# The second and third bf16 parts of layer 0's Q and K: VectorE instead of GpSimd, in a two-layer transformer kernel

## What is computed

```python
# layer 0, for x (8, 512, 256) and condition (8, 256)
mod = silu(condition) @ Wada + bada
sh_a, sc_a, gt_a, sh_m, sc_m, gt_m = split(mod, 6)
xm = layernorm(x, g1, be1) * (1 + sc_a) + sh_a
x  = x + gt_a * (causal_attention(xm @ Wqkv, 16 heads) @ Wproj + bproj)
xm = layernorm(x, g2, be2) * (1 + sc_m) + sh_m
x  = x + gt_m * (gelu(xm @ W1 + b1) @ W2 + b2)
# layer 1, for hidden = x and w = condition
h  = sln(hidden, w)                      # gamma(w) * layernorm(hidden) + beta(w)
q, k, v = h @ Wqkv.T + bqkv              # 16 heads, no mask
out = (softmax(q @ k.T) / 16) @ v @ Wp.T + bp
h1 = out + hidden
result = sln(h1, w) + h1
```

## Time and profile before

| what | value |
|---|---|
| median of three runs | 1229.31 us |
| lowest, highest | 1226.33, 1229.5 us |
| the profiled execution's own time | 1228.83 us |
| its span, first to last instruction | 1227.1 us |
| PE busy | 1167.0 us (95%) |
| DVE busy | 849.4 us (69%) |
| ACT busy | 656.0 us (53%) |
| POOL busy | 280.1 us (23%) |

### The profile page before, as it was taken

How to read it: one execution, slowest core, us unless ns; L and a number is a source line. 1 busy time by engine, 2 the same in 40 slices (tenths; PEclk the granted TensorE clock), 3 DMA queues, 4 the chain that set the end, 5 groups by cost and what they waited for, 6 DMA issues and landing times.

```text
span 1227.1 us, 17995 instructions
## 1 busy us (share of the span) xinstructions
PE 1167.0 (95%) x6462; PEld 587.2 (48%) x6462; DVE 849.4 (69%) x1620; ACT 656.0 (53%) x1184; POOL 280.1 (23%) x379
## 2 busy tenths in 40 slices
PE   9888999999999999999999999999999999999996
PEld 6444644454444634455445643446445463445333
DVE  4835689448984688826987388855798468764784
ACT  1262355746456555556565465565645655653664
POOL 1232221302331113301242013320232101310012
PEclk8899999999899999999999998999989999999998
DMA  5503032304232052300523023320323204300401
GB/s 201 175 9 96 21 119 39 104 18 117 56 90 66 18 137 62 102 26 30 156 56 103 19 76 93 81 78 19 110 59 87 72 1 126 80 18 16 116 20 43
DMA packets 59186, 89.31 MB, mean 73 GB/s; under 512 B 12914, under 2 KB 23762, under 8 KB 59098
## 3 DMA queue, kind: packets, MB, share of 16 engines
q1 hardware_dynamic: 57550, 86.83, 25.3%
q10 hardware_dynamic: 1548, 1.33, 0.4%
HBM read 24.41 MB, written 4.70 MB: 24 GB/s over the span
## 4 chain that ended last, share of the span: by engine, by line
PE 71%; DVE 15%; SPq 5%; ACT 4%; DMA 3%; issue 2%; POOL 1%; ACTq 0%; DVEq 0%; POOLq 0%
PE X L1097 16%; PE OP L993 12%; PE X L1028 10%; PE SC L1005 10%; PE X L1154 9%; PE X L1128 8%; DVE MX L797 6%; SPq L440 4%; ACT E L656 2%; DVE XN L847 2%; PE X L1031 2%; PE X L1112 1%; DVE PART L883 1%; DMA RS<-OE 1%; DVE STAT L804 1%
## 5 line engine op out<-in xcount | busy, mean ns | idle before, releaser
L797 DVE TENSOR_REDUCE MX<-X 128x1 f32<-128x512 f32 (+3 forms) x864 | 516.4, 660 | 170.3 <-PE X L1031 100.8
L656 ACT ACTIVATE E<-SC 128x512 f32<-128x512 f32 (+1 forms) x864 | 438.6, 592 | 278.0 <-PE SC L1005 238.0
L1028 PE MATMUL X<-KS,QS 96*128 96x512 bf16 (+3 forms) x1024 | 278.5, 349 | 16.6 <-DVE MX L797 11.6
L1005 PE MATMUL SC<-QS,KS 99*128 99x512 bf16 (+3 forms) x1024 | 261.3, 343 | 15.8 <-ACT E L656 11.1
L993 PE MATMUL OP<-E,V 128*32 128x512 f32 (+3 forms) x2048 | 212.3, 531 | 0.7 <-POOL E L565 0.4
L1005 PEld LDWEIGHTS SC<-QS,KS 99*128 99x128 bf16 x1024 | 89.7, 98 | 170.4 <-ACT E L656 89.1
L1028 PEld LDWEIGHTS X<-KS,QS 96*128 96x128 bf16 x1024 | 93.0, 98 | 147.5 <-DVE MX L797 67.4
L565 POOL TENSOR_SCALAR_AFFINE_SELECT E<-E 128x512 f32<-128x512 f32 x128 | 90.8, 717 | 223.9 <-ACT E L656 223.9
L1154 PE MATMUL X<-XT,W 128*128 128x512 f32 x256 | 117.0, 602 | 1.2 <-ACT XT L687 1.2
L1128 PE MATMUL X<-XT,WQKV 128*128 128x512 f32 x256 | 115.8, 596 | 1.3 <-ACT XT L687 1.2
L1097 PE MATMUL X<-W,HID 128*128 128x256 f32 x512 | 114.0, 380 | 0.1
(11 more groups left out here) (96 smaller groups left out, 936.7 us busy)
## 6 DMA issues: line engine op xcount, KB each, us to landing
QS<-PART SPq DMA_DIRECT2D x192, 128.0 KB, 2.4
KS<-PART SPq DMA_DIRECT2D x192, 128.0 KB, 2.5
OC<-OE SPq DMA_DIRECT2D x56, 128.0 KB, 3.9
RB<-recip_sums SPq DMA_DIRECT2D x56, 128.0 KB, 2.6
ROW<-row_vectors SPq DMA_DIRECT2D x8, 512.0 KB, 3.8
XIN<-in_x SPq DMA_DIRECT2D x7, 512.0 KB, 4.9
out<-OUT SPq DMA_DIRECT2D x7, 512.0 KB, 2.9
W<-in_w SPq DMA_DIRECT2D x2, 1024.0 KB, 6.7
```

The source lines that it names most:

```text
L656: a.activation(E[:, at["tick"].index() % 3, heads, lo:T], SC[(at["head"].index() + j) % 3][:, 0:len(banks[j]) * (T - lo)] .rearrange("p (h ...
L797: v.reduce_max(MX[:, qt, heads], psum.rearrange("p (h k) -> p h k", k=w), AX.X, negate=True)\
L1005: ins = t_.matmul(SC[(at["head"].index() + j) % 3][:, cols], KS[stacks(layer, b)][0:ALL_ROWS, 4 * g + h, kt * P:kt * P + P], QS[stacks(lay ...
L1028: ins = t_.matmul(bank[:, h * w:h * w + w], QS[stacks(layer, b)][0:CUT_ROWS, heads.start + h, qt * P:qt * P + P], KS[stacks(layer, b)][0:C ...
```

## The change

POOL's branch for `q0` and `k0` is gone. DVE now makes the second and third part in every case: after its two subtractions it rounds `X32` to `PART[:, side, 1]` and subtracts, and goes on in its list only then. The counts on the semaphores are as before; L598 and L600 are no more, L881 and L883 run for all eight elements of layer 0 and all eight of layer 1. (In the changed program every line behind the removed ones has a lower number, by 8 up to the removed condition and by 9 after it.)

```diff
--- before.py
+++ after.py
@@ -590,14 +590,6 @@
                     wait(pool, norm_dve, at["norm"].at(4, 4))
                     g.tensor_tensor(XR[:], XR[:], ROW0[:, 3:4, :].to_broadcast([P, TT, D]), ALU.add)\
                         .then_inc(bias_pool, 1)
-                elif what in ("q0", "k0") and b > 0:
-                    part = PART[:, "qk".index(what[0]), :, :, :]
-                    c = at["low"]
-                    wait(pool, dense_dve, at["by_dve"].at(1, 2))
-                    wait(pool, cut_low, c.at())
-                    g.tensor_scalar(part[:, 1], X32[:], 1.0, 0.0, ALU.mult, ALU.add).then_inc(cut_low, 1)
-                    wait(pool, cut_low, c.at(1, 1))
-                    g.tensor_tensor(part[:, 2], X32[:], part[:, 1], ALU.subtract).then_inc(cut_low, 1)
                 elif what.startswith("nm") :
                     m = at["maxima"]
                     cut, mx, mr = cut_maxima(what)
@@ -876,11 +868,10 @@
                                                          BQK1[:, 2 * side + t:2 * side + t + 1],
                                                          part[:, 0, t, :], ALU.add, ALU.subtract)
                         ins.then_inc(dense_dve, 1)
-                    if what[1] == "1" or b == 0:
-                        wait(dve, dense_dve, at["by_dve"].at(1, 2))
-                        v.tensor_copy(part[:, 1], X32[:]).then_inc(cut_low, 1)
-                        wait(dve, cut_low, at["low"].at(1, 1))
-                        v.tensor_tensor(part[:, 2], X32[:], part[:, 1], ALU.subtract).then_inc(cut_low, 1)
+                    wait(dve, dense_dve, at["by_dve"].at(1, 2))
+                    v.tensor_copy(part[:, 1], X32[:]).then_inc(cut_low, 1)
+                    wait(dve, cut_low, at["low"].at(1, 1))
+                    v.tensor_tensor(part[:, 2], X32[:], part[:, 1], ALU.subtract).then_inc(cut_low, 1)
```

## The result

The changed kernel takes 1254.12 us (median of 4 runs, 1249.53 to 1258.74) against 1228.15 (1226.33 to 1229.5) for the kernel before beside it: a ratio of 1.0214 with a 95% interval of 1.0181 to 1.0246. It is slower by 26 us; the forecast was 1250 with a range of 1236 to 1262. Its profiled execution took 1251.07 us.

A forecast was written before the change was run, and what follows sets the result against it. The prediction took PE, with 71% of the chain, to bound the kernel. It summed 14.75 - 3.1 + 1.95 + 1.65 - 0.2 = +15.05 on 1228.83 to 1243.9, plus 6 for the clock: 1250 us, range 1236 to 1262.

The forecast's parts named there:

- What bounds the kernel, and that the price of the pair does not decide: Whole kernel: PE holds 71% of the chain; its waits count, not the pair's 3.17 us on POOL against 1.92 on DVE.
- q0 in RING, 2.95 us a place: At RING's five q0, hold1's POOL addition blocks DVE's subtraction, delaying reductions and PE: 2.95 us each, +14.75.
- The lower bound, 0.9 without the block: At RING's q0, if the subtraction were not blocked, PE's late scans would cost 0.9 us a place.
- k0 in RING, -0.62: At RING's five k0, norm_m runs without POOL beside it and ends 0.62 us earlier: -3.1 in all.
- nearly gone: Sign expected in the changed kernel's profile: PE's wait before the transposes at k0, 1.32 us before, nearly disappears.
- Element 1, -0.2: At element 1, the pair delays proj0's DVE instructions, L916's block goes and k0 gives 0.6: -0.2 us together.
- Element 2, +1.95 at q0: At element 2's q0, the pair shifts DVE's unbroken reductions, PE's scans and the V product by 1.95 us.
- Element 2, +1.65 at k0: At element 2's k0, norm_m precedes the pair, reductions start 1.95 us later and up_0 waits for a bank: +1.65.
- The sum without the clock, +15.05: All places together, clock falls left out: +15.05 us on the profiled 1228.83, giving 1243.9.
- The clock, +6: New PE waits at RING's q0 make the granted clock fall two or three times, at 2.5 us a fall: +6.
- the block does not happen: Rival at RING's q0: DVE's subtraction is not blocked, 5 x 0.9 replaces 14.75, no clock falls: 1233.6; chance 0.09.
- Faster, hidden by DVE's slack: Rival: DVE's idle time, chiefly at q0, hides the pair, leaving only k0's gain: 1225.1; chance 0.06.

The follow-up runs named there:

- experiment 2: The kernel before, with only k0's second and third part moved to DVE and q0's left on POOL: 1226.96 us, ratio 0.999 to the kernel before.
- experiment 3: The kernel before, with only q0's second and third part moved to DVE and k0's left on POOL: 1252.73 us, ratio 1.0207 to the kernel before.
- experiment 1: The changed kernel, with hold1's POOL addition also waiting for Q's second and third part: 1234.18 us, ratio 1.0057 to the kernel before.
- experiment 5: The changed kernel, with hold1's POOL addition replaced by a memset of RH that reads nothing: 1233.36 us, ratio 1.0056 to the kernel before.

## Why the prediction was right

- **What bounds the kernel, and that the price of the pair does not decide:** right. Experiments 2 and 3 move the same work, once for nothing and once for 26 us.
- **q0 in RING, 2.95 us a place:** 2.91 in every place without a fall of the clock. Each step stands in the rows: POOL released behind the rounding and ahead of the subtraction, a subtraction of 3.27 us (forecast near 3.4), reductions at once behind it, the V product moved by what the fifth reduction is late. The lower bound, 0.9 without the block, was measured in experiment 1: 0.88.
- **k0 in RING, -0.62:** -0.62 in all ten places of the two profiles. I forecast PE's wait before the transposes "nearly gone"; the bracket went from 1.32 to 0.27.
- **Element 1, -0.2:** -0.36 and -0.14.
- **Element 2, +1.95 at q0:** the first late scan is 1.99 us late; the rest of the 3.12 is a fall of the clock that I had counted at no place but RING's `q0`.
- **Element 2, +1.65 at k0:** too small (and its own sum, 226.06 less 224.44, gives 1.62). The step that failed is the one that took the pair for 1.95 us there. I had asked at each `q0` which POOL instruction would run beside the pair, and not at this `k0`. The wait is about 2.4 us with the block of 0.65, and a fall of the clock makes it 4.1.
- **The sum without the clock, +15.05:** the places without the falls give 5 x 2.91 - 3.1 - 0.36 + 1.95 + 2.4 = +15.4.
- **The clock, +6:** right as a sum, wrong in its parts, so the closeness of the total is in part luck. I took two or three falls at RING's `q0` at 2.5 us each. There were three and four, at 1.0 us each (3.9 against 2.91); the rest, 1.2 and 1.7 us, came at element 2. My price came from a fall of another length: the one at 745 kept the clock at half for 6.8 us, each at these `q0` for 3.4. Where a fall at `q0` did last 6.8 us, in the kernel with only Q on VectorE, the place cost 5.51, which is 2.6 more than 2.91. That the same 3.4 us cost 1.0 at `q0` and 1.7 at element 2's `k0` I put down to the reductions, which space PE's scans at `q0` anyway; no run tests that. A fall at `q0` of the first pass of RING in the changed kernel, then the long one (columns as in rows 9):

```profile
360.00:362.00 2.00, 0.06 (x1) 0.06 (x2) 2.00 (x3) 0.27 (x1) 0.20 (x1) 1.00 0.03 9
362.00:364.00 2.00, 2.00 (x5) 0.66 (x6) 2.00 (x4) 1.03 (x3) 0.00 (x0) 0.51 0.00 0
364.00:366.00 2.00, 2.00 (x9) 0.61 (x11) 2.00 (x4) 1.14 (x3) 0.00 (x0) 0.64 0.00 0
```

```profile
648.00:650.00 2.00, 1.50 (x4) 0.58 (x5) 2.00 (x4) 0.42 (x1) 0.00 (x0) 0.60 0.00 0
650.00:652.00 2.00, 2.00 (x6) 0.60 (x4) 1.99 (x4) 1.44 (x4) 0.00 (x0) 0.50 0.00 0
652.00:654.00 2.00, 2.00 (x10) 0.40 (x12) 2.00 (x4) 0.31 (x1) 0.00 (x0) 0.50 0.15 49
654.00:656.00 2.00, 2.00 (x14) 0.41 (x7) 0.56 (x1) 0.00 (x0) 0.00 (x0) 0.69 0.60 200
```

- **The rivals:** "the block does not happen" is excluded as a description of the change. Its price was +4.8 us; where experiments 1 and 5 made it so, the medians were 7.5 and 7.1 us above the kernel before. Element 2 costs 3.6 us above its two terms, which is enough for the difference. "Faster, hidden by DVE's slack" fails where I said it would, at the first reduction.

What stays open is why the clock falls at one `q0` and not at the next, and why for 3.4 us or for 6.8: the waits there are alike (2.08 and 2.09 us), and no kernel was made to tell them apart. The two groups of runs of the changed kernel, 1254 and 1249, differ by no more than a few such falls would make, which is a reading and not a test.

## What to carry to other kernels

Before work goes from GpSimd to VectorE because it is shorter there, ask which GpSimd instruction comes forward into the gap and what VectorE runs at that moment. In these traces a VectorE instruction with two SBUF inputs (1.23 us, then 3.27), a rounding from float32 to bf16 (0.69, then 1.34) and a scaling within SBUF (0.41, then 2.29) each waited until a GpSimd instruction that reads SBUF was done. Where such a pair meets on the path, order is worth more than the engine: one wait turned a loss of 23 to 26 us into 7.5, and one wait in the original, which let VectorE's short instructions go first, gained 15.

## What I had not expected of the hardware

- A GpSimd memset of 128 x 1024 (1.41 us, of which 0.46 was waiting) did not hold up a VectorE subtraction with two SBUF inputs, but was itself held up by a float32-to-bf16 rounding on VectorE.
- DVE's VE works on 4 elements a partition, and was held up until POOL's addition of 2.36 us was done all the same: 1.30 us instead of 0.17.
- PE lost 2.27 us at a place where its rows showed 1.59 us of waiting. The difference of two traces at the same matmul tells the loss, the brackets alone do not.
- Falls of the granted clock to half came in two lengths at the same kind of place: 3.4 us, at a cost of 1.0 us, and 6.8 us, at a cost of 2.6.
